# One-hot tiles of a histogram and an adjacency build, with two steps side by side in place of eight or sixteen

## The reference, cut to what matters

```python
ones_e = jnp.ones(edge_src.shape[0], dtype=features.dtype)
deg_out = jax.ops.segment_sum(ones_e, edge_src, num_segments=N)      # the histogram
norm_out = jax.lax.rsqrt(jnp.maximum(deg_out, 1.0))
h = (features * norm_out[:, None]) @ W
agg = jax.ops.segment_sum(h[edge_src], edge_dst, num_segments=N)     # uses the built matrix
```

## Time and profile before

| what | value |
|---|---|
| time before, median of 3 runs | 2855.87 us (2855.09 to 2861.72) |
| the profiled execution: its own time | 2854.37 us |
| the profiled execution: span in the trace | 2852.7 us |
| histogram | 27 to 63 us |
| matrix build, b = 0 to 16, no product beside it | 67 to 110 us |
| matrix build, b = 17 to 146, with the first product | 110 to 434 us |
| rest of the first product | 434 to 455 us |

### The profile page before, as it was taken

One profiled execution on the slowest core, in us unless ns is written; L12 is line 12 of the kernel. 1 busy time (PEld: TensorE's weight loads), 2 busy tenths in 40 slices (PEclk: granted clock), 3 DMA queues, 4 the chain that ended last, 5 costly groups with the idle time before them and its releaser, 6 DMA issues.

```text
span 2852.7 us, 33483 instructions
## 1 busy us (share of the span) xinstructions
PE 2108.9 (74%) x10859; PEld 1483.5 (52%) x10859; DVE 1430.3 (50%) x3094; ACT 966.7 (34%) x2148; POOL 1366.6 (48%) x1417
## 2 busy tenths in 40 slices
PE   5899999558888886737777777754444444499998
PEld 4677777247777774523333333443333343266666
DVE  8877673746777665734444444332222222612424
ACT  4533331423333332834444443332222222301202
POOL 3000000667777773577777772457777774300000
PEclk6799999879898886868888887775655555699999
DMA  9599852279999983137777775325555554465461
GB/s 214 171 329 341 310 198 75 81 211 264 265 258 264 269 251 105 27 92 244 240 237 237 244 238 164 84 57 124 138 130 136 132 133 97 165 202 169 130 203 35
DMA packets 518583, 517.97 MB, mean 182 GB/s; under 512 B 153344, under 2 KB 463763, under 8 KB 517227
## 3 DMA queue, kind: packets, MB, share of 16 engines
q1 hardware_dynamic: 310349, 267.63, 30.9%
q0 software_dynamic: 50528, 115.22, 15.9%
q10 hardware_dynamic: 157534, 132.98, 15.1%
HBM read 301.53 MB, written 227.32 MB: 185 GB/s over the span
## 4 chain that ended last, share of the span: by engine, by line
POOL 37%; PE 33%; issue 15%; DVE 9%; DMA 4%; ACT 2%; POOLq 0%; SPq 0%; ACTq 0%; DVEq 0%
POOL arena L1049 34%; PE ps L1586 10%; PE ps L1488 7%; PE ps L1474 5%; PE ps L1568 2%; PE ps L1679 1%; DVE arena L1997 1%; PE ps L1857 1%; DMA arena<-t_attn,src_i 1%; PE ps L1705 1%; DVE arena L2457 1%; DMA arena<-t_gat,src_i 1%; ACT arena L1080 1%; PE ps L1847 1%; POOL starts_q L1000 1%
## 5 line engine op out<-in xcount | busy, mean ns | idle before, releaser
L1080 ACT ACTIVATE arena<-ps 128x774 f32<-128x774 f32 (+8 forms) x689 | 494.4, 730 | 1200.0 <-PE ps L1679 655.1
L1049 POOL DMA_INDIRECT arena<-t_gat,src_i x784 | 740.5, 944 | 239.0 <-issue 236.8
L1679 PE MATMUL ps<-arena 128*128 128x136 f32 (+2 forms) x2352 | 688.5, 454 | 89.6 <-DVE arena L2347 83.0
L1679 PEld LDWEIGHTS ps<-arena 128*128 128x128 f32 x2352 | 462.2, 259 | 238.5 <-DVE arena L2347 114.6
L1049 POOL DMA_INDIRECT arena<-t_attn,src_i x392 | 383.0, 977 | 126.7 <-issue 113.4
L1637 PE MATMUL ps<-ident,logit 128*64 128x128 f32 (+2 forms) x147 | 47.2, 321 | 384.5 <-DVE logit L2308 313.3
L1586 PE MATMUL ps<-arena 128*128 128x384 bf16 x1850 | 306.3, 329 | 33.5 <-DVE rec L2504 31.4
L2295 DVE TENSOR_TENSOR z_b<-arena 128x12 f32<-128x12 f32 (+1 forms) x196 | 34.0, 173 | 587.6 <-DMA arena<-t_gat,src_i 580.4
L1586 PEld LDWEIGHTS ps<-arena 128*128 128x128 bf16 x1850 | 182.3, 99 | 157.2 <-issue 40.2
L1488 PE MATMUL ps<-arena 128*128 128x100 bf16 x1176 | 239.8, 362 | 10.0 <-DVE arena L2127 9.0
L1637 PEld LDWEIGHTS ps<-ident,logit 128*64 128x64 f32 (+2 forms) x147 | 14.1, 96 | 429.4 <-DVE logit L2308 350.3
(11 more groups left out here) (321 smaller groups left out, 2764.1 us busy)
## 6 DMA issues: line engine op xcount, KB each, us to landing
ends_gat<-arena ACTq DMA_DIRECT2D x98, 774.0 KB, 4.1
arena<-adj_hbm SPq DMA_DIRECT2D x90, 640.0 KB, 3.9
same_b<-same_hbm SPq DMA_DIRECT2D x294, 128.0 KB
adj_hbm<-arena SPq DMA_DIRECT2D x9, 3200.0 KB, 12.1
ends_attn<-arena ACTq DMA_DIRECT2D x98, 272.0 KB, 4.8
ends_gat<-arena ACTq DMA_DIRECT2D x98, 258.0 KB, 3.7
arena<-edst SPq DMA_DIRECT2D x98, 256.0 KB, 5.0
starts_q<-zrow SPq DMA_DIRECT2D x28, 896.0 KB, 6.9
```

The costliest lines, as they stand in the source:

```text
L1049: g.indirect_dma_start(out=row_b[:, n % RB, k, 0:row_tab[p].shape[1]], out_offset=None, in_=row_tab[p], in_offset=bass.IndirectOffsetOnAxi ...
L1080: return a.activation(o, i, ACT.Copy)
L1679: i = mm(o, same_f[:, g % RB, k, :], msg[:, g % 4, k * W:(k + 1) * W], start=True, stop=True)
```

## The change

The one-hot tiles get the order (pair of steps, index, two steps): each index has the values of two neighbouring steps side by side, and the next index follows at once. So the weights or moving columns of one step lie 2 elements (4 bytes) apart. `iota_two` holds each index twice. VectorE writes the same tiles with as many instructions of as many elements; its iota operand is repeated over the pairs of steps and its value operand over the indices. A `room` keeps the later tiles at their addresses.

```diff
-        work = carve(arena, {"iota_rep": (P, (P, BATCH), BF16), ...
-                             "hot_e": (P, (3, P, BATCH), BF16), "hot_k": (P, (3, KEYS, BATCH), BF16),
+        work = carve(arena, {"iota_two": (P, (P, 2), BF16), "room": (P, (P * (BATCH - 2) // 2,), F32), ...
+                             "hot_e": (P, (3, BATCH // 2, P, 2), BF16), "hot_k": (P, (3, BATCH // 2, KEYS, 2), BF16),
...
-        hists = carve(arena, {"hot_lo": (P, (2, P, WIDE), BF16), "hot_hi": (P, (2, NT, WIDE), BF16)}, hist_at)
+        hists = carve(arena, {"hot_lo": (P, (2, WIDE // 2, P, 2), BF16), "hot_hi": (P, (2, WIDE // 2, NT, 2), BF16)}, hist_at)
...
-                    i = mm(bank(7)[:, 0:NT], hot_lo[:, slot, :, k], hot_hi[:, slot, :, k],
+                    i = mm(bank(7)[:, 0:NT], hot_lo[:, slot, k // 2, :, k % 2], hot_hi[:, slot, k // 2, :, k % 2],
...
-                    i = mm(ps[:, at:at + KEYS], hot_e[:, b % 3, :, e], hot_k[:, b % 3, :, e], start=True, stop=True)
+                    i = mm(ps[:, at:at + KEYS], hot_e[:, b % 3, e // 2, :, e % 2], hot_k[:, b % 3, e // 2, :, e % 2], start=True, stop=True)
...
-            v.tensor_copy(iota_rep[:, :, :], bc(iota_i[:, :].rearrange("p (i a) -> p i a", a=1), [P, P, BATCH]))
+            v.tensor_copy(iota_two[:, :, :], bc(iota_i[:, :].rearrange("p (i a) -> p i a", a=1), [P, P, 2]))
...
+            def one_hot(o, parts, values):
+
+                n = o.shape[1]
+                return tt(o, bc(iota_two[:, 0:parts, :].rearrange("p (a i) s -> p a i s", a=1), [P, n, parts, 2]),
+                          bc(values.rearrange("p (a i s) -> p a i s", i=1, s=2), [P, n, parts, 2]), ALU.is_equal)
...
-                    i = tt(o[:, slot, :, 0:r * BATCH].rearrange("p i (a k) -> p i a k", a=r),
-                           bc(iota_rep[:, 0:parts, :].rearrange("p i (a k) -> p i a k", a=1), [P, parts, r, BATCH]),
-                           bc(k[:, at:at + r * BATCH].rearrange("p (i a k) -> p i a k", i=1, a=r), [P, parts, r, BATCH]),
-                           ALU.is_equal)
+                    i = one_hot(o[:, slot, 0:r // 2, :, :], parts, k[:, at:at + r])
...
-                tt(hot_e[:, b % 3, :, :], iota_rep[:, :, :], bc(lo.rearrange("p (a s) -> p a s", a=1), [P, P, BATCH]),
-                   ALU.is_equal)
-                tt(hot_k[:, b % 3, :, :], iota_rep[:, 0:KEYS, :],
-                   bc(key.rearrange("p (a s) -> p a s", a=1), [P, KEYS, BATCH]), ALU.is_equal).then_inc(hot_done, 1)
+                one_hot(hot_e[:, b % 3, :, :, :], P, lo)
+                one_hot(hot_k[:, b % 3, :, :, :], KEYS, key).then_inc(hot_done, 1)
```

More of the change, by code:

```diff
@@ L362, in gnn_stack_kernel @@
         cmp, val_i, val_f = (look[k] for k in ("cmp", "val_i", "val_f"))
-        work = carve(arena, {"iota_rep": (P, (P, BATCH), BF16), "lo_t": (P, (NC, P), BF16), "key_t": (P, (NC, P), BF16),
-                             "hot_e": (P, (3, P, BATCH), BF16), "hot_k": (P, (3, KEYS, BATCH), BF16),
+        work = carve(arena, {"iota_two": (P, (P, 2), BF16), "room": (P, (P * (BATCH - 2) // 2,), F32), "lo_t": (P, (NC, P), BF16), "key_t": (P, (NC, P), BF16),
+                             "hot_e": (P, (3, BATCH // 2, P, 2), BF16), "hot_k": (P, (3, BATCH // 2, KEYS, 2), BF16),
                              "dst_row": (P, (UNROLL, GC, P), I32)}, work_at)
-        iota_rep, lo_t, key_t, hot_e, hot_k, dst_row = (
-            work[k] for k in ("iota_rep", "lo_t", "key_t", "hot_e", "hot_k", "dst_row"))
+        iota_two, lo_t, key_t, hot_e, hot_k, dst_row = (
+            work[k] for k in ("iota_two", "lo_t", "key_t", "hot_e", "hot_k", "dst_row"))
         block_i = dst_row[:, 0, :, :].rearrange("p k e -> p (k e)")[:, 0:CH]
         hist_at = work_at + P * BATCH // 2 + NC * P
-        hists = carve(arena, {"hot_lo": (P, (2, P, WIDE), BF16), "hot_hi": (P, (2, NT, WIDE), BF16)}, hist_at)
+        hists = carve(arena, {"hot_lo": (P, (2, WIDE // 2, P, 2), BF16), "hot_hi": (P, (2, WIDE // 2, NT, 2), BF16)}, hist_at)
         hot_lo, hot_hi = hists["hot_lo"], hists["hot_hi"]
@@ L1989, in _ @@
             ts(brk_r[:, :, :], brk_r[:, :, :], -BIG, None, ALU.mult).then_inc(s_bits, 1)
+            def one_hot(o, parts, values):
+                n = o.shape[1]
+                return tt(o, bc(iota_two[:, 0:parts, :].rearrange("p (a i) s -> p a i s", a=1), [P, n, parts, 2]),
+                          bc(values.rearrange("p (a i s) -> p a i s", i=1, s=2), [P, n, parts, 2]), ALU.is_equal)
             def hot(turn):
                 slot, at = turn % 2, turn * WIDE
-                r = min(WIDE, CH - at) // BATCH
+                r = min(WIDE, CH - at)
                 if turn >= 2:
```

## The result

The changed kernel takes 2822.73 us, the median of four runs (2818.55 to 2827.0), beside 2856.69 us for the kernel before on the same chip: a ratio of 0.9879, with a 95% interval of 0.9867 to 0.9891. That is 34 us faster, where 53 were forecast. The profiled execution took 2818.55 us, and its span fell from 2852.7 to 2816.9 us.

A forecast was written before the change was run, and what follows sets the result against it. VectorE was taken to bound the histogram, TensorE the build from 110 us, three fifths of it strided matmuls. Savings of 0.3 + 1 + 10.6 + 16 + 25 = 53 us gave 2803 us, range 2780 to 2842.

The forecast's parts named there:

- small parts: Histogram 0.3 us saved, 67 to 110 us 1 us saved, from 434 us on nothing.
- TensorE's pace: Build, line 1488: a 100-column matmul goes from 183 to 60 ns, with 49 and 100 ns also considered.
- VectorE's one-hots: Histogram and build: comparisons cost no change, 693 ns for 1024 and 570 ns for 800 elements.
- rival of slower one-hots: Histogram and build: comparisons fall to one element a cycle, 2937 us; 13 in 100, 6 of them for a milder 2883.
- 16 were taken: Build during the zero fill, 151 to 323 us: DMA limits it to 156 us, 16 saved (0 to 27).
- 156 us of the forecast: Time taken for the build's 69 batches during the zero fill, between 145 and today's 172 us.
- 25 were taken: Build after 323 us: 44 batches save 29 us, less 2 us for each of two chunks, so 25.
- 2 us for each of two chunks: Build after 323 us: stall taken off where a chunk stands in the queue ahead of a row of destinations.
- early batches: Build before 151 us: 16 batches save 10.6 us, and 67 to 110 us saves 1 us.
- sum for the build (52.6): Build savings together: 1 + 10.6 + 16 + 25 us, without the histogram's 0.3.
- The clock: Build: TensorE's clock falls because of gaps, granted 0.83, giving 2829 us; 10 in 100.
- DMA doesn't hold it: Build: all 130 batches run at 1.82 us, 86 + 1 us saved, 2769 us; 4 in 100.
- the pace stays: Build: strided matmuls stay at 183 ns because the step was not the cost, 2856 us; 5 in 100.

The follow-up runs named there:

- one pause: Changed kernel with VectorE's third histogram turn waiting for TensorE's turn 1 instead of turn 0: 2804.9 us, ratio 0.9814.
- three-slot kernel: Kernel before, old layout, with three histogram one-hot buffers instead of two, so VectorE waits for the turn three back: 2875.09 us, ratio 1.0073.
- fastest kernel: Changed kernel plus VectorE's pause, 14 of 28 zero-fill parts issued behind the last chunk, and each chunk stored in four parts: 2776.17 us, ratio 0.972.

## Why the forecast was right in sign, and where it went wrong

**The step that failed** is one of the small parts: "In the histogram VectorE stays the bound; only the eight steps behind its last comparison get shorter". VectorE did stay the bound, but this costed TensorE's faster turns at nothing else, and looked at nobody besides VectorE and TensorE. What was missing is GpSimd, whose gathers need a break in VectorE's comparisons; the wait on `s_hist` behind slow turns had given it one. It was worth +18.6 us to the first one-hot, +20 us alone, and one pause of 0.74 us gives it back. With it the kernel takes 2804.9 us, 2 from the forecast. That this agrees so well is partly luck: the next points show terms that were off by 2 and 4 us in opposite directions, and falls of the clock that the sum had left out.

The row of 2.83 us beside its neighbours of 1.1 us stood in the trace before, and it was not asked what it waited for. VectorE's break before the change is too short (0.02 to 0.04 us) to stand in its timeline as idle time; it shows in the distance of the starts, and the three-slot kernel, in which it is gone, shows that the gather hung on it.

The Trainium skill has a rule near this (SBUF — State Buffer, Who interferes with whom): VectorE and GpSimd share a pair of ports as an exclusive lock, and a VectorE instruction with two inputs in SBUF contends there with a GpSimd instruction that reads SBUF. It adds, as inferred, that such an instruction doesn't touch the generation of descriptors, which needs the write side. In these runs a gather is held for 26.8 us beside comparisons of that kind, so the measurement speaks against the inference for a whole gather. But 18 others ran beside the same comparisons at 1.1 us each in the kernel before; which access is held, and why only one gather's, no run here shows.

**TensorE's pace.** 60 ns were taken, 49 measured; the dense end of the bounds was right. As the forecast said, it hardly matters.

**VectorE's one-hots** cost 684 and 568 ns, 693 and 570 before, and 1220 for 2048 elements. The rival of slower one-hots is refuted: a repeated word costs nothing here, also as the first operand.

**The build by its parts.** A batch is 8 matmuls and 6.25 of the product, so the counts in the windows give the pace. The same two stretches before the change, from the first to the last issue of the fill and from there to the tail:

```profile
149.23:327.89 178.66, 178.66 (x1020) 128.97 (x1019) 131.92 (x260) 60.59 (x73) 0.00 (x0) 1.00 0.98 345
327.89:434.23 106.34, 106.34 (x607) 76.72 (x606) 73.02 (x135) 35.16 (x42) 0.00 (x0) 1.00 0.63 224
```

During the fill it is now 1030 / 14.25 = 72.3 batches in 162.1 us, 2.24 us each; before, 2.50. That saves 18 us where 16 were taken (0 to 27). The bytes are the same, 61.6 MB and 61.7 before, and the rate is 380 GB/s; the 156 us of the forecast meant 384 for its somewhat shorter window (which held 26 of the 28 parts and not all). So this term was right, its rate too. Behind the fill, 580 / 14.25 = 40.7 batches take 80.3 us, 1.97 each: 21 us saved where 25 were taken. There VectorE waited 9.1 us in three waits for rows, up to 5.2 us, where 2 us for each of two chunks were taken. The rest, 51.4 - 18 - 21 = 12 us, are the early batches, 11.6 by the forecast. So the sum for the build (52.6) met 51.4 by its mechanism, with two terms that were a little off in opposite directions.

**The clock.** It was a rival with 10 in 100, and it came in part: a granted 0.92 during the fill and 0.87 behind it, against 1.00 before. After a wait of 5.24 us for a row, which ended at 355.6 us, the windows read:

```profile
355.00:365.00 10.00, 7.53 (x56) 4.94 (x57) 9.37 (x19) 3.04 (x4) 0.00 (x0) 0.66 0.63 209
365.00:375.00 10.00, 9.43 (x94) 6.26 (x93) 10.00 (x20) 5.22 (x7) 0.00 (x0) 1.00 0.76 226
```

In the first the mean lies between the two levels, 1.2 and 2.4 GHz; in the second it is back. In the fastest kernel, whose waits for rows are at most 3.0 us, it stays at 0.97 to 1.00 from 150 us on, while TensorE is busy for 40 to 42 of 50 us. In the changed kernel, from 130 us to the tail, TensorE is idle eight times for 2.5 to 8.1 us behind a late row, and the clock is at its lower level eight times, each time from within or right behind one of these. So here the falls come with the long waits and not with the gaps of every batch. What they cost by themselves was not measured.

**DMA doesn't hold it** is refuted by the share of 1.04 and by the fill's 22 us; **the pace stays** by the 49 ns.

## What to carry to other kernels

When an engine gets faster, look not only at what it waits for but at who lives in the short stops that its slowness caused elsewhere: a third engine may need them, even if they last only 0.03 us, and a row that is longer than its neighbours (here 2.83 us among 1.1) is where to ask. After such a change, look again at transfers that were hidden while another engine was the bound: moving half of the fill was worth nothing before and 11 to 24 us after. And place them short of the next stage's loads in the same queue, for the whole fill behind them cost 34 us of waiting for weights.

## What was not expected of the hardware

- A gather on GpSimd (2.83 us at most before) is held for 26.8 us by uninterrupted bf16 comparisons on VectorE, through turn 18, up to its next other instructions. A break of 0.02 to 0.04 us releases it as one of 0.74 us does, and the gather ends within 1 us of the start of either (at 30.76 us, where VectorE goes on at 29.87, and at 30.95, where it stops at 29.98). It happens in both layouts and with either operand first.
- Once one gather has got in, the next ones run beside the same comparisons at 1.1 us each without VectorE stopping. Why, stays open.
- A matmul's pace with 100 columns goes from 183 to 49 ns when the step of both its weights and its moving columns falls from 16 to 4 bytes, and by the forecast's dense pace (49 ns) 4 bytes cost no more than dense. Which of the two operands the old step cost was not tested.
